# Reading a conditioned tile's lower parts from its PSUM bank instead of its copy

## The reference

```
w      = weights[itok[b]]                          # 128 x 128, one of 32
c      = w^T x[b]                                  # conditioning: 128 x 2048
result = c @ W_base^T + b_base                     # 2048 x 2048
h      = c @ A^T (8 experts x 16), logits = c @ W_gate^T
out[b] = x[b] + result + SCALING * sum_e route_e(logits) * (h_e @ B_e^T)
```

## Time and profile before

| | us |
|---|---|
| median of 3 runs | 1578.25 |
| lowest, highest | 1577.69, 1579.81 |
| the profiled execution | 1579.12 |
| its span in the trace | 1577.3 |
| TensorE busy | 1506.0 (95%) |
| VectorE busy | 1352.3 (86%) |
| ScalarE busy | 626.1 (40%) |
| GpSimd busy | 640.5 (41%) |

### The profile page before, as it was taken

One profiled execution on the slowest core, in us unless ns is written; L12 is line 12 of the kernel. 1 busy time (PEld: TensorE's weight loads), 2 busy tenths in 40 slices (PEclk: granted clock), 3 DMA queues, 4 the chain that ended last, 5 costly groups with the idle time before them and its releaser, 6 DMA issues.

```text
span 1577.3 us, 25817 instructions
## 1 busy us (share of the span) xinstructions
PE 1506.0 (95%) x9411; PEld 808.5 (51%) x9411; DVE 1352.3 (86%) x2257; ACT 626.1 (40%) x1026; POOL 640.5 (41%) x508
## 2 busy tenths in 40 slices
PE   4678999999999999999989999999999999999998
PEld 4554554555455555555545455555455555455553
DVE  6788999999899999999968888888888888888875
ACT  6864444444543445434413332223332323332321
POOL 2565555666665555665522122122122122122122
PEclk9899999999999999999999999999999999999999
DMA  6234555655555555655797333344333344433342
GB/s 232 94 132 156 163 165 173 191 166 161 150 176 167 161 168 178 177 179 157 227 339 247 108 123 101 99 141 126 116 121 91 111 141 123 118 116 94 114 111 74
DMA packets 169567, 235.95 MB, mean 150 GB/s; under 512 B 71898, under 2 KB 88794, under 8 KB 167130
## 3 DMA queue, kind: packets, MB, share of 16 engines
q1 hardware_dynamic: 167426, 219.63, 46.0%
q10 hardware_dynamic: 2016, 14.68, 2.4%
HBM read 147.83 MB, written 86.43 MB: 149 GB/s over the span
## 4 chain that ended last, share of the span: by engine, by line
PE 73%; DVE 11%; issue 4%; POOL 2%; DMA 1%; ACT 1%; SPq 0%; DVEq 0%; ACTq 0%; POOLq 0%
PE bank_x L1427 8%; PE bank_x L1429 8%; PE bank_x L1428 8%; PE bank_y L1427 8%; PE bank_y L1429 8%; PE bank_y L1428 8%; PE bank_z L1427 3%; PE bank_z L1429 3%; PE bank_z L1428 3%; PE bank_h L1427 2%; PE bank_h L1429 2%; PE bank_h L1428 2%; PE bank_c L1427 2%; DVE t_sums L1070 2%; PE bank_c L1429 2%
## 5 line engine op out<-in xcount | busy, mean ns | idle before, releaser
L602 POOL TENSOR_TENSOR x_res<-x_res,t_sums 128x512 f32<-128x512 f32 x255 | 350.5, 1377 | 843.4 <-DVE t_sums L1075 684.1
L1427 PE MATMUL bank_y<-TT,s_parts 128*128 128x512 f16 x768 | 292.1, 380 | 4.7 <-DVE TT L1185 4.2
L1427 PE MATMUL bank_x<-TT,s_parts 128*128 128x512 f16 x768 | 292.9, 381 | 1.3 <-DVE TT L1185 1.3
L1428 PE MATMUL bank_x<-TT,s_parts 128*128 128x512 f16 x768 | 292.5, 381 | 0.0
L1429 PE MATMUL bank_x<-TT,s_parts 128*128 128x512 f16 x768 | 292.3, 381 | 0.0
L1429 PE MATMUL bank_y<-TT,s_parts 128*128 128x512 f16 x768 | 291.9, 380 | 0.0
L1428 PE MATMUL bank_y<-TT,s_parts 128*128 128x512 f16 x768 | 291.9, 380 | 0.0
L710 ACT ACTIVATE p_copies<-bank_x,y_inv 128x512 f32<-128x512 f32 x128 | 87.7, 685 | 417.7 <-PE bank_x L1429 307.3
L1075 DVE TENSOR_TENSOR t_sums<-t_sums,inv_w 128x512 f32<-128x512 f32 x255 | 233.8, 917 | 8.7
L1045 DVE TENSOR_TENSOR s_parts<-a_full,s_parts 128x512 f16<-128x512 f32 x224 | 192.9, 878 | 33.0 <-ACT s_parts L695 33.0
L574 POOL TENSOR_TENSOR x_res<-x_res,BT 128x512 f32<-128x512 f32 x128 | 206.9, 1616 | 26.3 <-DMA x_res<-in_x_dram 23.3
(11 more groups left out here) (243 smaller groups left out, 2750.5 us busy)
## 6 DMA issues: line engine op xcount, KB each, us to landing
x<-in_x_dram SPq DMA_DIRECT2D x32, 1024.0 KB, 5.8
x_res<-in_x_dram SPq DMA_DIRECT2D x128, 256.0 KB, 4.0
part_scratch<-x_res SPq DMA_DIRECT2D x128, 256.0 KB, 3.0
x_res<-part_scratch SPq DMA_DIRECT2D x128, 256.0 KB, 3.9
out_dram<-x_res SPq DMA_DIRECT2D x128, 256.0 KB, 3.0
wt_scratch<-late_words SPq DMA_DIRECT2D x64, 224.0 KB, 3.4
TT<-wt_scratch ACTq DMA_DIRECT2D x14, 1024.0 KB, 8.3
x_parts<-in_L_ffn_W_base_dram SPq DMA_DIRECT2D x18, 512.0 KB, 6.4
```

Of the source, the lines that this page charges most:

```text
L602: nc.gpsimd.tensor_tensor(XR[:, xr_slot(m), :], XR[:, xr_slot(m), :], TM[:, m % 2, :], ALU.add).then_inc(r_added, 1)
L1427: nc.tensor.matmul(dst, lhs[0], rhs[0], start=start, stop=False, skip_group_check=chained)
L1428: nc.tensor.matmul(dst, lhs[0], rhs[1], start=False, stop=False, skip_group_check=chained)
```

## The change

The lower parts of A11, A12 and A22 of steps 1 to 16 (those that are conditioned in the first pass) are computed as bank * Y_DOWN - upper part, with a scalar_tensor_tensor that reads bank_c, instead of AF - upper part, with a tensor_tensor that reads SBUF twice. So bank_c may be written again only after them: the conditioning of S1 waits for A11's lower part, that of A22 for A12's, and the transpose of the next maxima, which also uses bank_c, for A22's. S1's lower part still comes from AF. In the loop, A11's lower part moves ahead of the first half's C21 and C22 (in the prologue its place is unchanged).

```diff
+        def from_bank(n, q):
+            return 0 < n <= NP and q in (A11, A12, A22)
...
             def s_lower(n, q):
                 dve.wait_ge(s_hi, n_s(n, q))
+                if from_bank(n, q):
+                    nc.vector.scalar_tensor_tensor(out=SO[:, slot(n, q), 1, :, :], in0=quads(BC[:, :]), scalar=Y_DOWN,
+                                                   in1=SO[:, slot(n, q), 0, :, :], op0=ALU.mult,
+                                                   op1=ALU.subtract).then_inc(s_lo, 1)
+                    return
                 nc.vector.tensor_tensor(SO[:, slot(n, q), 1, :, :], quads(AF[:, af_of[q], :]), SO[:, slot(n, q), 0, :, :],
                                         ALU.subtract).then_inc(s_lo, 1)
...
+                if not second:
+                    s_lower(n + 1, A11)
                 finish(n, 0, C21)
                 finish(n, 0, C22)
...
                 if not second:
-                    s_lower(n + 1, A11)
                     s_lower(n + 1, S1)
                     sum_s2(n + 1)
                     s_lower(n + 1, A12)
...
             def cond(n, u):
...
+                if from_bank(n, A11) and u in (U_S1, U_A22):
+                    pe.wait_ge(s_lo, n_s(n, A11 if u == U_S1 else A12))
...
             def transpose_maxima(n):
...
+                if from_bank(n - 1, A22):
+                    pe.wait_ge(s_lo, n_s(n - 1, A22))
```

## The result

| | before | after |
|---|---|---|
| median, us | 1578.91 (1577.69 to 1579.81, 4 runs) | 1613.57 (1611.16 to 1614.03, 4 runs) |
| profiled execution, its span | 1579.12, 1577.3 | 1613.63, 1611.8 |
| ratio | | 1.0217 [1.0205, 1.0229] |

A forecast was written before the change was run, and what follows sets the result against it. TensorE, busy 95% of the span, was taken as the bound. Stalls at A22 of 23.7, step 8's 3.0 and step 1's 2.9 made 29.6 us on 1578.25: 1607.8 us, sum's range 1603 to 1612, outer bounds 1596 to about 1615.

The forecast's parts named there:

- The release of the bank: A22's conditioning on TensorE must wait for VectorE's A12 lower part: 23.7 us over thirteen steps.
- Not given back: VectorE's gained time goes into idling some 3.4 us ahead of C11, so it does not offset the new stalls.
- A11 free in the gap: A11's lower part, 0.68 us, fits VectorE's idle time ahead of C21: cost zero, up to 0.2 us in steps like 11.
- steps like 10: Steps 3, 5, 7, 10, 12, 14: TensorE's stall at A22's conditioning, 1.43 us each.
- steps like 11: Steps 2, 4, 6, 9, 11, 13, 15: TensorE's stall at A22's conditioning, 2.16 us each.
- step 1: S1's matmuls wait 2.86 us for A11's lower part, which follows C11; A22's wait there is covered.
- 0.24 "brought along": In steps like 10, VectorE carries 0.24 us from the step before, lowering the A22 stall from 1.67 to 1.43.
- rival 1: New stalls swallow the old waits before conditionings and step 1's share: +18.4 us, about 1597; chance 0.10.
- Step 8: The step building four chunks of weights: TensorE waits at S1 and A22, 1.9 to 3.5 us, taken as 3.0.
- Step 16 and the boundary: The same 2.2 us stall, followed by VectorE's 4.79 us wait for a DMA of x; counted 0, at most 2.2.
- Clock: Rival: longer TensorE waits bring one or two falls of the granted clock, adding 2 to 5 us: 1612; chance 0.06.
- Rival 2: Faster: S1 and the S2 sum fall from 1.68 to 0.60 us without GpSimd's adds beside them, no stall: 1570; chance 0.03.

The follow-up runs named there:

- The last run of the experiments: Changed kernel with step 1 as before, A22's conditioning one product later, S2's lower part and the S4 sum ahead of C11: 1579.76 us, ratio to before 1.0003.
- the run with the waits alone: Changed kernel with its order and all new waits kept, but the lower parts of A11, A12 and A22 read AF as before: 1629.78 us, ratio to before 1.0319.

## Why the prediction was right, and where its terms were off

**The release of the bank** was the right mechanism, shown from both sides: without A12's wait 27.1 us go, with a later A22 all 34.7. **Not given back** held as well: VectorE idles 3.60 us ahead of C11 where some 3.4 were said, and the seven waits on the weights' split stay at 7.1 us. **A11 free in the gap** held in the steps like 10; in the steps like 11 there is a stall of 0.27 us at S1, a little over the 0.2 that was allowed for. It was left out of the sum because the later wait covers it, and the total there bears that out (next list). The price of **0.68 from a bank** held to 2 ns; the 65 ns more that were estimated by the Trainium skill ("VectorE: DVE Perf Modes", section on the TRN2 errata) are not in the 48 instructions (676 to 692 ns, against a median of 684 for the copy). From step 10 to step 11 it is 46.5 us from A22 to A22, as said. Part of the closeness of the total is luck: step 1 and the steps like 10 came 5.6 us over their terms, and step 9 came 1.6 under.

The terms that were mis-sized:

- *Steps like 10* (3, 5, 7, 10, 12, 14), 1.43 said, 1.88 measured, +2.7 in six. In step 10 the A12 part ends 8.07 us after C21's start (552.21 - 544.14) where 7.93 were taken (529.70 - 521.77): C21's second instruction took 1.38 for 1.25, held up more by an add. The release took 0.14 us instead of 0.06 (552.21 to 552.35), +0.08. The 0.24 "brought along" were not there: C12 had been late, but C21 waits for its product in either case (0.43 idle ahead of it), so nothing could be carried past it. That step of the reasoning was wrong and could have been read from the 1.15 us idle ahead of C21.
- *Steps like 11* (2, 4, 6, 9, 11, 13, 15), 2.16 said, 2.2 to 2.4 measured, but put together otherwise: some 1.98 at A22 and 0.27 at S1. In step 9 only 0.6 are left. The stall is there, but the stretch from step 8's A22 to step 9's A11 took 36.16 us before and 34.51 now: TensorE's waits on VectorE in it (2.4 before, 1.0 after) shrank, as rival 1 has it. It came true in this one place.
- *Step 1*, 2.9 said, 5.8 measured: a stall of 2.4, a fall of the clock behind it of 1.7, and another 1.7 us at half clock ahead of the first changed instruction. That last part isn't shown to be the change's: up to there the kernel with A12 from its copy has the same instructions and its A11 conditioning starts at 124.09, as before (125.81 in after). The last run of the experiments leaves step 1 as before and starts it at 125.69, with the same granted clock of 0.57 from 118 to 126 us as in after. So two kernels with nothing changed up to there show both values.
- *Step 8*, 3.0 said, 3.4 measured, put together otherwise: the S1 wait grew from 1.83 to 3.59, 1.7 us of half clock stood behind it, and at A22 there was no stall, since S1's delay had let VectorE catch up. The 1.7 at half clock is no fixed part of it: behind the same wait of 3.6 us there was none in the kernel with A12 from its copy.
- *Step 16 and the boundary*: +3.2 (2.0 at A22, 0.3 at S1 and 1.0 more at A11) and -3.5. The wait on the way to the DMA of x absorbed it, as said, and a little more: the wait of 4.68 became 2.11, with no fall of the clock behind it, and the 6.8 us at half clock became 3.4, behind the next wait.
- *Clock*, a rival with 0.06: it came true on top of the sum, twice (behind the waits of 2.26 and 3.59 us), 3.4 us. Its price of 2 to 5 was right and its chance too small. The wait of 4.68 that it rested on was not the only long one in the trace of before: one of 4.18 ends at 119.80, and the clock is 0.66 from 120 to 125 us. A wait of 2.64, the one on diag_inv, had no fall behind it there (window 140 to 147 above), so the rows left open what one of 2.3 would do.

Rival 1 came true in one place, with 1.6 us. Rival 2's condition was met only where half of GpSimd's adds were taken away, and there by half. What stays open is when a wait lets the clock fall. Half clock follows the wait on diag_inv (2.55 to 3.54 us) in after and in ten experiments, but not in before (2.64) nor in before without the bias (2.80). It follows the wait of 3.6 us in step 8 in every run that has one, for 3.4 or 6.8 us, except in the kernel with A12 from its copy. No run varied such a wait alone.

## What to carry to other kernels

Before an instruction is pointed at another source to make it cheaper, put the end of its last reader beside the moment at which that source is written again: here the copy let the bank go 3.3 to 3.8 us before VectorE was done, and the 1.68 us taken out of VectorE's queue didn't buy that back in any of fourteen steps. A saving on an engine that idles later in the same step goes into that idle time; what could be had was to fill the idle time (1576.92) and not to make the queue shorter. And where two engines take turns at SBUF as here, an instruction taken out of the row can hand its turn to the next one, so that the gain is one undisturbed duration and not the stretched one, unless the turns themselves go.

## What the runs showed of the hardware

- A bank read with one SBUF input took 676 to 692 ns in all 48 cases. In 30 of them a GpSimd instruction ran beside it, in 15 for its whole length, at 677 or 678 ns. The form with two SBUF inputs takes 1.75 us there, and removing one such instruction stretched the next from 0.68 to 1.75.
- Released by s_lo, TensorE started 0.14 us after VectorE's end (552.21 to 552.35, and alike in the other steps with such a stall); released by the weights' split in step 11 it took 0.06.
- The granted clock fell to the 1.2 GHz level for 3.4 us behind waits of TensorE of 2.26 and 3.59 us in after. In the thirteen steps with stalls of 1.9 to 2.0 us (2 to 7, 9 to 15) it stayed at 1.00 (windows 160 to 450 and 475 to 815 us, both 1.00).
- The length of a wait did not decide it alone. Behind waits of 3.10 to 3.13 us in the run with the waits alone the clock fell in four steps (3, 5, 7, 10) and not in two (12, 14); behind one of 3.58 it stayed at 1.00 with A12 from its copy; behind one of 1.99 (862.00) it fell in after. At the pass boundary before, it was 0.51 from 820 to 827, around the end of the wait of 4.68.
